# Edge counts kept in memory by pairs of source tiles: 512-byte store runs, single-tile loads, whole-pair transposes

## The reference, cut to what matters

```python
h = jnp.maximum(_layernorm(x, axis=-1), 0.0)
x = x + _L0_gnn_ref(h, src, dst, edge_weight, ...)   # weighted sum over edges of gated rows: the build below
h = jnp.maximum(_layernorm(x, axis=-1), 0.0)
x = x + _L1_gnn_ref(h, edge_index, ...)              # sum of h[src] into dst              (pass 1)
h = jnp.maximum(_layernorm(x, axis=-1), 0.0)
x = x + _L2_gnn_ref(h, edge_index, ...)              # sum of messages into dst            (pass 2)
h = jnp.maximum(_layernorm(x, axis=-1), 0.0)
x = x + _L3_gnn_ref(h, edge_index, hyperedge_weight, ...)
# inside L3: e_feat = B_inv * segment_sum(h[row], col)      (pass 3)
#            out    = D_inv * segment_sum(e_feat[col], row) (pass 4: the same edges, turned round)
#            then a batch norm over the nodes, relu
```

## Time and profile before

| | |
|---|---|
| median of three runs | 2806.36 us |
| the profiled execution | 2810.06 us |
| its span | 2808.3 us |
| mean granted TensorE clock | 0.963 of full speed |
| TensorE matmuls busy | 2372.3 us, 84% of the span |
| VectorE busy | 1654.4 us, 59% |
| ScalarE busy | 1241.9 us, 44% |
| moved by DMA | 603.26 MB in 1784416 packets |

### The profile page before, as it was taken

The page is one execution under the profiler, slowest core; times in us unless marked ns, Lnnn a source line. Parts: engine busy times, 40 slices in busy tenths (PEclk is TensorE's granted clock), DMA queues, the critical chain, the costliest instruction groups (busy, mean ns, idle before and its releaser), DMA issues. The chain is left out here.

```text
span 2808.3 us, 73414 instructions
## 1 busy us (share of the span) xinstructions
PE 2372.3 (84%) x27975; PEld 2020.1 (72%) x27975; DVE 1654.4 (59%) x3900; ACT 1241.9 (44%) x2708; POOL 66.2 (2%) x60
## 2 busy tenths in 40 slices
PE   1435799988898889898885799989999999999996
PEld 0323677777777777777774688878888788887774
DVE  5278799989898999898896233323334211211114
ACT  0514677777777777677673322222222100011113
POOL 0350000000000000000000000000000000000000
PEclk9999999999999999999897899999999999999997
DMA  9611999999999999999999899999999999999994
GB/s 277 190 46 33 204 198 202 195 191 202 191 206 187 208 191 201 193 182 198 182 189 211 207 278 276 276 248 251 254 251 256 245 290 290 279 242 253 247 252 119
DMA packets 1784416, 603.26 MB, mean 215 GB/s; under 512 B 1258086, under 2 KB 1781098, under 8 KB 1784093
## 3 DMA queue, kind: packets, MB, share of 16 engines
q1 hardware_dynamic: 1782538, 594.63, 99.1%
q0 software_dynamic: 1600, 4.92, 0.6%
HBM read 276.78 MB, written 109.03 MB: 137 GB/s over the span
## 5 line engine op out<-in xcount | busy, mean ns | idle before, releaser
L1074 ACT CAST stage<-ps 128x784 f16<-128x784 f32 x784 | 654.7, 835 | 205.7 <-PE ps L539 98.7
L584 PE MATMUL ps<-Ha,a_pairs 128*128 128x258 f16 x4802 | 548.4, 274 | 46.6 <-ACT Ha L1120 39.0
L584 PEld LDWEIGHTS ps<-Ha,a_pairs 128*128 128x128 f16 x4802 | 470.1, 98 | 116.8 <-ACT Ha L1120 39.2
L537 PE MATMUL ps<-hot_c,hot_r 128*128 128x98 f16 x3136 | 512.3, 213 | 12.6 <-DVE hot_c L797 7.4
L538 PE MATMUL ps<-hot_c,hot_r 128*128 128x98 f16 x3136 | 506.4, 211 | 0.0
L539 PE MATMUL ps<-hot_c,hot_r 128*128 128x98 f16 x3136 | 505.2, 211 | 0.0
L1057 ACT CAST stage<-ps 128x392 f16<-128x392 f32 x784 | 397.1, 507 | 208.0 <-PE ps L520 207.9
L512 PE MATMUL ps<-g_in,wt 128*128 128x128 f16 x2401 | 438.9, 225 | 46.1 <-DVE X L809 32.4
L513 PE MATMUL ps<-g_in,wt 128*128 128x128 f16 x2401 | 435.8, 223 | 0.0
L514 PE MATMUL ps<-g_in,wt 128*128 128x128 f16 x2401 | 435.3, 223 | 0.0
L809 DVE SCALAR_TENSOR_TENSOR X<-ps,X 128x512 f32<-128x512 f32 (+1 forms) x637 | 393.3, 657 | 17.6 <-PE ps L514 16.9
(11 more groups left out here) (190 smaller groups left out, 2202.3 us busy)
## 6 DMA issues: line engine op xcount, KB each, us to landing
a_pairs<-counts_by_source SPq DMA_DIRECT2D x75, 3136.0 KB, 14.1
counts_by_source<-stage SPq DMA_DIRECT2D x50, 1568.0 KB, 9.4
edge_table<-src_pad SPq DMA_DIRECT2D x1, 6464.0 KB, 27.8
edge_table<-dst_pad SPq DMA_DIRECT2D x1, 6464.0 KB, 49.6
edge_table<-w_pad SPq DMA_DIRECT2D x1, 6464.0 KB, 47.7
gated_parts<-G SPq DMA_DIRECT2D x1, 3136.0 KB, 12.6
g_in<-gated_parts SPq DMA_DIRECT2D x98, 32.0 KB, 3.3
out_x<-X SPq DMA_DIRECT2D x6, 512.0 KB
```

The source lines that it names most:

```text
L537: mm(into(0), rows_, codes(0), start=v == 0, stop=True, skip_group_check=True)
L584: last = mm(ps[:, c % 2, 0:PARTS], a_slot(ph, c, i), moving[:, i], start=i == 0, stop=i == TILES - 1)
L1074: a.copy(stage[:, b, 0:2, :, u * SET_COLS:(u + 1) * SET_COLS], of).then_inc(s("hi_done"), 1)
```

## The change

The count matrix lies in memory by pairs of source tiles: `counts_by_source` has the shape (25 pairs, 128 partitions, 49 destination tiles, 2, 128), where it had (49, 128, 50 x 128). For one destination tile, the counts of source tiles 2i and 2i+1 are now neighbours, 512 bytes together. `stage` gets a 50th source tile, which ScalarE sets to zero once for each side before the build. The store of a tile writes 25 runs of 512 bytes from each partition, where it wrote 49 of 256 bytes. The extra store after tile 0 and its waits are gone. Passes 1 to 3 load one destination tile at a time (1600 KB, 25 runs of 512 bytes for each partition) into a ring of six tiles, `a_tiles`, and wait for each one. Pass 4 issues one DMA transpose for two source tiles, 98 blocks of 128 x 128 from rows that follow each other in memory, 25 transposes in all, into a ring of three pairs. The last pair is tile 48 and the zero tile.

```diff
-FIRST_HALF = -(-TILES // 2)
+FULL = TILES + TILES % 2
...
-def pair_at(ph, c):
-
-    return (ph - 1) * FIRST_HALF + c // 2
+def load_at(ph, c):
+
+    return (ph - 1) * TILES + c
+
+
+def pair_at(c):
+
+    return (c // 2 + 2) % (SLOTS // 2)
...
-        by_source = nc.dram_tensor("counts_by_source", (TILES, P, (TILES + 1) * P), F16).ap()
+        by_source = nc.dram_tensor("counts_by_source", (FULL // 2, P, TILES, 2, P), F16).ap()
...
-        stage, o = at("stage", [P, 2, 1 + WEIGHTS, TILES, P], F16, o)
+        stage, o = at("stage", [P, 2, 1 + WEIGHTS, FULL, P], F16, o)
...
-        a_pairs, _ = at("a_pairs", [P, SLOTS // 2, TILES, 2, P], F16, o)
-        a_turned, o = at("a_turned", [P, SLOTS, TILES, P], F16, o)
+        a_turned, _ = at("a_turned", [P, SLOTS // 2, TILES, 2, P], F16, o)
+        a_tiles, o = at("a_tiles", [P, SLOTS, FULL, P], F16, o)
...
             if ph == 4:
-                return a_turned[:, c % SLOTS, i]
-            return a_pairs[:, pair_at(ph, c) % 3, i, c % 2]
+                return a_turned[:, pair_at(c), i, c % 2]
+            return a_tiles[:, load_at(ph, c) % SLOTS, i]
+
+        def two_tiles(j):
+
+            cols = by_source.rearrange("i p j a d -> p i j (a d)")
+            return cols[:, :, j] if isinstance(j, int) else cols[:, :, bass.ds(j, 1)].rearrange("p i j n -> p i (j n)")
...
-            eng.wait_ge(s("filled"), 16)
...
-                    cols = slice(j * P, (j + 1) * P) if isinstance(j, int) else bass.ds(j * P, P)
-                    sp.dma_start(by_source.rearrange("i p n -> p i n")[:, :, cols], stage[:, b, 0]).then_inc(s(f"stored{b}"), 16)
-                    if isinstance(j, int) and j == 0:
-
-                        sp.dma_start(by_source.rearrange("i p n -> p i n")[:, :, TILES * P:], stage[:, b, 0]).then_inc(s("filled"), 16)
+                    sp.dma_start(two_tiles(j), stage[:, b, 0].rearrange("p (i a) d -> p i (a d)", a=2)).then_inc(s(f"stored{b}"), 16)
...
-                        if ph == 4:
+                        q = load_at(ph, c) % SLOTS
+                        if ph < 4:
                             if later(j, SLOTS):
-
-                                sp.wait_ge(s("sum_done4"), j - (SLOTS - 1))
-                            else:
-                                sp.wait_ge(s("sum_done3"), min(TILES, 46 + c // 2 * 2))
-                            sp.dma_start_transpose(a_turned[:, c % SLOTS], slab(by_source, j)[:, 0:TILES * P]).then_inc(s(f"turned_in{c % SLOTS}"), 16)
+                                sp.wait_ge(s(f"sum_done{ph}"), j - (SLOTS - 1))
+                            elif ph > 1:
+                                sp.wait_ge(s(f"sum_done{ph - 1}"), TILES - SLOTS + 1 + c)
+                            sp.dma_start(a_tiles[:, q].rearrange("p (i a) d -> p i (a d)", a=2), two_tiles(j)).then_inc(s(f"a_in{q}"), 16)
                         elif c % 2 == 0:
                             if later(j, SLOTS):
 
-                                sp.wait_ge(s(f"sum_done{ph}"), j - (SLOTS - 2))
-                            elif ph > 1:
-                                sp.wait_ge(s(f"sum_done{ph - 1}"), min(TILES, 46 + c))
-                            q = pair_at(ph, c) % 3
-                            rows = by_source.rearrange("i p n -> p i n")
-                            cols = slice(j * P, (j + 2) * P) if isinstance(j, int) else bass.ds(j * P, 2 * P)
-                            sp.dma_start(a_pairs[:, q].rearrange("p i a d -> p i (a d)"), rows[:, :, cols]).then_inc(s(f"a_in{q}"), 16)
+                                sp.wait_ge(s("sum_done4"), j - (SLOTS - 2))
+                            else:
+                                sp.wait_ge(s("sum_done3"), min(TILES, TILES - 3 + c))
+                            rows = by_source.rearrange("i p j a d -> i p (j a d)")
+                            pair = rows[c // 2] if isinstance(j, int) else rows[bass.ds(k * (SLOTS // 2) + c // 2, 1)].rearrange("i p n -> (i p) n")
+                            sp.dma_start_transpose(a_turned[:, pair_at(c)].rearrange("d j a p -> d (j a) p"), pair).then_inc(s(f"turned_in{pair_at(c)}"), 16)
...
-                            if isinstance(j, int) and j == 2:
-                                act.wait_ge(s("filled"), 16)
...
                     act.wait_ge(s("g_stored"), 16)
+                    for b in range(2):
+                        a.activation(stage[:, b, 0, TILES], minus16[:], ACT.Copy, scale=0.0)
```

More of the change, by code:

```diff
@@ L244, in gnn_kernel @@
         acc, g = at("acc", [P, TILES, WIDE], F32, base0 + 60 * 1024)
-        assert base0 + 60 * 1024 >= base0 + 32000 + TILES * P * 4 and g <= base0 + 2 * TILES * PARTS * 2 + SLOTS * TILES * P * 2
+        assert base0 + 60 * 1024 >= base0 + 32000 + TILES * P * 4 and g <= base0 + 2 * TILES * PARTS * 2 + SLOTS * FULL * P * 2
         rows_all, g = at("rows_all", [P, TILES, WIDE], F32, g)
-        assert g <= base0 + 2 * TILES * PARTS * 2 + SLOTS * TILES * P * 2
+        assert g <= base0 + 2 * TILES * PARTS * 2 + SLOTS * FULL * P * 2
         picked, g = at("picked", [P, WIDE], F32, o)
@@ L338, in hand_on @@
                         sp.dma_start(g_in[:, b, part], slab(g_dram, j)[:, part]).then_inc(s(f"g_loaded{b}"), 16)
-                        sp.dma_start_transpose(wt[:, b, a], stage[:, b, 1 + a].rearrange("p i d -> p (i d)")).then_inc(s(f"wt_in{b}"), 16)
-                    cols = slice(j * P, (j + 1) * P) if isinstance(j, int) else bass.ds(j * P, P)
-                    sp.dma_start(by_source.rearrange("i p n -> p i n")[:, :, cols], stage[:, b, 0]).then_inc(s(f"stored{b}"), 16)
-                    if isinstance(j, int) and j == 0:
-                        sp.dma_start(by_source.rearrange("i p n -> p i n")[:, :, TILES * P:], stage[:, b, 0]).then_inc(s("filled"), 16)
+                        sp.dma_start_transpose(wt[:, b, a], stage[:, b, 1 + a, 0:TILES].rearrange("p i d -> p (i d)")).then_inc(s(f"wt_in{b}"), 16)
+                    sp.dma_start(two_tiles(j), stage[:, b, 0].rearrange("p (i a) d -> p i (a d)", a=2)).then_inc(s(f"stored{b}"), 16)
                 tiles_loop(sp, hand_on, 0)
@@ L519, in take_high @@
                     o = ps[:, 2 * unit_at(c, u) + 1, 0:HALF * WCOLS].rearrange("p (i x) -> p i x", i=TILES)
-                    mm(o, minus16[:], stage[:, b, 1, :, u * SET_COLS:(u + 1) * SET_COLS], start=False, stop=True, skip_group_check=True).then_inc(s("low_left"), 1)
+                    mm(o, minus16[:], stage[:, b, 1, 0:TILES, u * SET_COLS:(u + 1) * SET_COLS], start=False, stop=True, skip_group_check=True).then_inc(s("low_left"), 1)
                 def half_windows(j, b, c, u):
@@ L575, in step @@
                             if ph == 4:
-                                pe.wait_ge(s(f"turned_in{q}"), (k + (c // SLOTS + 1)) * 16)
+                                pe.wait_ge(s(f"turned_in{pair_at(c)}"), (k + (c // SLOTS + 1)) * 16)
                             else:
-                                pe.wait_ge(s(f"a_in{pair_at(ph, c) % 3}"), (k + (pair_at(ph, c) // 3 + 1)) * 16)
+                                pe.wait_ge(s(f"a_in{load_at(ph, c) % SLOTS}"), (k + (load_at(ph, c) // SLOTS + 1)) * 16)
                             if later(j, 2):
@@ L1056, in low_parts @@
                     of = ps[:, 2 * unit_at(c, u) + 1, 0:HALF * WCOLS].rearrange("p (i x) -> p i x", i=TILES)
-                    a.copy(stage[:, b, 2, :, u * SET_COLS:(u + 1) * SET_COLS], of).then_inc(s("lo_done"), 1)
+                    a.copy(stage[:, b, 2, 0:TILES, u * SET_COLS:(u + 1) * SET_COLS], of).then_inc(s("lo_done"), 1)
                 def build(j, k, c):
@@ L1073, in build @@
                         of = ps[:, bank:bank + 2, 0:HALF * WCOLS].rearrange("p k (i x) -> p k i x", i=TILES)
-                        a.copy(stage[:, b, 0:2, :, u * SET_COLS:(u + 1) * SET_COLS], of).then_inc(s("hi_done"), 1)
+                        a.copy(stage[:, b, 0:2, 0:TILES, u * SET_COLS:(u + 1) * SET_COLS], of).then_inc(s("hi_done"), 1)
                 if not general:
                     act.wait_ge(s("g_stored"), 16)
+                    for b in range(2):
+                        a.activation(stage[:, b, 0, TILES], minus16[:], ACT.Copy, scale=0.0)
                     tiles_loop(act, build, 0)
```

1 line of the change is left out of this document (added).

## The result

The changed kernel takes 2727.12 us, median of four executions (2721.72 to 2733.95), where the kernel before took 2806.66 beside it on the same chip, also four (2797.59 to 2816.75). The ratio is 0.9716, with a 95% interval of 0.9682 to 0.975: 79.5 us less. The forecast was 2750 us, 57 less. It was right in direction, and the time lies within the range for eight in ten (2713 to 2795 us). The profiled execution took 2727.58 us, its span is 2725.8.

A forecast was written before the change was run, and what follows sets the result against it. Store chains bound the build, TensorE passes 1 to 3, transposes pass 4. Gains 32 + 9 + 16 = 57 us took the profiled 2810.06 to 2753, put at 2750 for the median; own range 2735 to 2770, eight in ten 2713 to 2795.

The forecast's parts named there:

- The store's movement: Build: 512-byte runs cut a store's movement from 7.2 to 5.65 us, about 1.7 less with instruction fetches.
- The store's worth: Build: shorter stores cut ScalarE's waits, gaining 32 us; bounds 0 and about 60.
- the 25 waits: Build: ScalarE's store waits beside tile 2's, 69.7 us in all; 25 x 1.7 x 0.75 = 32 us saved.
- The extra store: Start of the build: without L344's store tile 2 starts earlier, gaining 9 us; bounds 6 to 13.
- these 0.8 us: Start of the build: allowance for the last count in the landing time of tile 0's store.
- Zeros, last store, single loads: Zero tile, build's last store and loads of passes 1 to 3: each forecast to change nothing.
- Rival C: Passes 1 to 3: single loads don't keep up, costing 79 us, so 2829; chance 0.08.
- Pair transposes: Pass 4: 25 transposes of 12.15 us each gain 16 us; bounds a loss of 4 and a gain of 24.
- the 0.93: Pass 4: of 6.47 us a tile, 0.93 us is what each transpose instruction costs beside 5.54 of movement.
- Rival A: Nearly all build stalls go and transposes stop binding pass 4: 93 us gained, 2713; chance 0.20.
- its bound of 60: Build: upper bound of the gain from shorter stores, about 60 us, used in A's 60 + 9 + 24.
- Rival B: Stores get no faster, or transposes keep their cost by block: 2785 to 2769, both 2805; chance 0.20.

The follow-up runs named there:

- e2: Changed kernel with each store of counts cut in two DMAs of 256-byte runs in the new layout; 0.9928 of the kernel before.
- e3: Changed kernel with an extra store of tile 0's counts (512-byte runs) and ScalarE's wait for it before tile 2; 0.9768 of the kernel before.
- e4: Changed kernel with each pair transpose of pass 4 cut into two instructions of 49 blocks; 0.9796 of the kernel before.
- e8: Kernel before, with SyncE issuing a tile's high transpose only after the store of the tile ahead has landed; 1.0108 of the kernel before.

## Why the prediction was right, and where it was too small

- **The store's movement.** Forecast: from 7.2 to 5.65 us, and the first cast 7.6 us after the issue. Measured: 292 GB/s in the stretch and 7.62 us at the tile shown; the shortest distance fell from 9.1 to 7.5. Right.
- **The store's worth, 32 us. This is the term that was mis-sized.** It measured 58 in the profiles and 55 to 59 in the times of `e2`. Two steps of the working failed. The first is the 25 waits at 1.7 us each, and three quarters of that. With the short runs back, ScalarE's waits beside tile 2's hold 94.0 - 8.3 = 85.7 us, and 46.3 - 6.6 = 39.7 without them: 46 us, not 32. A store that a transpose joins lands another 1.6 us late, and the shorter one mostly escapes that. The second is to count visible waits alone: 12 of the 58 us are no such wait. Where they lie can be read, though no run tests it. Over tiles 3 to 46 the time from a tile's last high cast to the next tile's first fell from 2.7, 3.0 and 3.0 us (three profiles before) to 2.0, and the time of a tile's own high casts from 22.7, 22.9 and 22.9 to 22.6, 22.5 and 22.5. The granted clock of the build was 0.96, 0.95 and 0.95 before, 0.97, 0.98 and 0.98 in the changed kernel: with shorter waits TensorE stands at the lower level for less of the time. That this is what shortens a tile's own casts is my reading. The 85.1 us of the earlier trace rows were also a low draw, since the two other profiles of the kernel before have 97.1 and 98.5.
- **The extra store, 9 us.** It costs 4 to 10 by `e3`. Without it tile 2's first cast comes 8.6 us after the store of tile 0 was issued, where the working had 7.85 (1.4 + 5.65 + 0.8); no run shows these 0.8 us by themselves.
- **Zeros, last store, single loads: nothing.** The loads keep up. Pass 3 holds 290 GB/s over 22 single loads without a gap, and takes the 270 us of the earlier trace rows. The loads' issues, 0.37 us each, stay hidden in a queue that still waits 670.7 us for sums. Rival C did not occur. By its own working it would have cost more than the change gives from 6.8 us a load, not from 6.7. The Trainium skill, DMA: Bandwidth & Descriptors, Anatomy of one DMA, gives a fixed 2.0 us for each DMA that GpSimd issues. These loads are issued by SyncE, and no such cost fell on the engines when their number doubled.
- **Pair transposes, 16 us.** The gain was 14 to 15. A pair takes 12.05 us (forecast 12.15), and the gain lies at the borders between instructions, as was taken; that their number and not the adjacency of the rows makes it is argued from the equal rates, since `e4` changed both. The part that goes with an instruction is smaller than the 0.93 worked out from an average over the pass: 2 x 6.34 - 12.05 = 0.63 us for each one spared. The gain fell short of 16 because TensorE, not the transposes, holds the last five tiles. The faster contiguous transpose that the Trainium skill, DMA: Bandwidth & Descriptors, Latency and other measured facts, speaks of isn't seen here: inside a transpose the rate was 290 GB/s with the rows apart and is 290 with the rows adjacent, and the measurement decides.
- **Rival A** had the right size for the store, its bound of 60, and one of its reasons was right: a store that lands before the next transpose begins no longer shares the engines with it. The event that it named didn't occur: the stalls didn't go (46.3 us remain in 25 waits), and the transposes still bind pass 4, if only just.
- **Rival B** asked whether stores of longer runs are no faster, or transposes cost by block. `e2` denies the first. For the second, 98 blocks in one instruction take 12.05 us and in two 12.7.

Corrected, the sum is 58 + 4 to 10 + 14.5, so 76 to 83, where the median shows 79.5 with an interval of about 9 us to each side, and the two later ratios of the changed kernel, 0.9731 and 0.9732, come to 76. What stays open is the start of the kernel, 22 to 23 us in some executions of either kernel, what delays the store of the first tile in a turn of the loop, and why two profiles of the kernel before had builds of 1249.6 us and one of 1223.6.

## What to carry to other kernels

Where one queue carries a chain of DMAs that returns buffers two tiles on, the visible waits times what one DMA saves is too low a price for it: here that gave 32 us, the waits alone fell by 46, and the whole was 58. Look at what joins the DMA in flight. Profile a kernel more than once before working from one trace, since its build spread over 26 us. Test a layout's effects apart, and look whether the edit keeps all the rest: here run length was worth 58 us and the pair transposes 14, and cutting the transposes in two also undid the adjacency of their rows. Before moving a transfer to another place or queue, ask whether the engines behind it are full, and what would bind next: here it was VectorE, 1.4 us a tile below.

## What the runs showed of the hardware

- Stores from the core in runs of 256 bytes moved 224 GB/s and, in the new layout, 217 (`e2`); in runs of 512 bytes 292, about as loads and transposes did (290).
- A DMA transpose that was issued while a store was still moving made the store land about 1.6 us later (10.9 instead of 9.3 us from issue to the cast it releases; 31 of 34 waits in `e8`).
- Transposes from core to core buffer beside a plain store of another queue landed after 13.8 us at the median instead of 11.0, and the store after 9.8 instead of 7.8.
- Transposes of 49 blocks started 6.34 us apart, those of 98 blocks 12.05: an estimate from the two is 0.6 us for each instruction beside its blocks.
- Inside a transpose from memory the rate was 290 GB/s, whether its rows were adjacent or not.
- After TensorE had stood idle for 4.45 us (second profile of the kernel before), the granted clock was 0.50 for the 3 us from 1241 to 1244.
- At the turns of the hardware loop, one tile in six, the first cast came some 3.5 us later than at other tiles (12.7 to 13.3 us after the store in the first profile of the kernel before, 11.4 to 11.9 in that of the changed one), with no DMA to wait for.
